# Moving the shift's store and loads to ScalarE's DMA queue, with a new placement of the pieces

## The reference

```
x = x + xattn(layernorm(x), ctx)      # 16 heads of 16: causal self-attention + cross-attention, one output projection
x = x + moe_ffn(layernorm(x))         # 8 experts; each takes the 512 tokens with its highest scores of all 4096
```

## Time and profile before

| | before |
|---|---|
| median of 3 runs | 1600.5 us (1596.9 to 1601.5) |
| the profiled execution | 1592.2 us |
| its span, first to last instruction | 1590.5 us |
| granted TensorE clock, mean | 0.949 |
| PE, DVE, ACT, POOL busy | 91%, 74%, 57%, 34% |
| waits of PE's weight loads for the shift | 31.5 us, 6 times |

### The profile page before, as it was taken

One profiled execution on the slowest core, in us unless ns is written; L12 is line 12 of the kernel. 1 busy time (PEld: TensorE's weight loads), 2 busy tenths in 40 slices (PEclk: granted clock), 3 DMA queues, 4 the chain that ended last, 5 costly groups with the idle time before them and its releaser, 6 DMA issues. The chain is left out here.

```text
span 1590.5 us, 25662 instructions
## 1 busy us (share of the span) xinstructions
PE 1453.4 (91%) x8560; PEld 702.0 (44%) x8560; DVE 1170.5 (74%) x3215; ACT 902.6 (57%) x1754; POOL 547.2 (34%) x1012
## 2 busy tenths in 40 slices
PE   8899999999899899989998999899989856999997
PEld 4443443444344344434443444344433323676674
DVE  6978888878788688879886988687877068455451
ACT  2177777667677677767775677567767600212211
POOL 4032333442344224432533252334113121444442
PEclk8599999999999999999998999899999977999999
DMA  6876473829373855566456736582810120345442
GB/s 176 116 128 106 89 108 103 116 67 142 101 97 87 133 113 87 101 136 106 78 118 127 101 86 110 102 113 70 124 22 3 41 84 14 94 116 122 104 110 51
DMA packets 82388, 155.22 MB, mean 98 GB/s; under 512 B 13008, under 2 KB 46416, under 8 KB 82256
## 3 DMA queue, kind: packets, MB, share of 16 engines
q1 hardware_dynamic: 74752, 142.43, 47.8%
q0 software_dynamic: 6144, 8.52, 3.2%
q10 hardware_dynamic: 1360, 2.62, 0.5%
HBM read 96.52 MB, written 53.08 MB: 94 GB/s over the span
## 5 line engine op out<-in xcount | busy, mean ns | idle before, releaser
L837 ACT ACTIVATE probs<-bank_ps 128x512 f32<-128x512 f32 (+1 forms) x1408 | 719.7, 581 | 273.7 <-PE bank_ps L628 268.9
L943 DVE TENSOR_REDUCE chunk_max<-bank_ps 128x1 f32<-128x512 f32 x1024 | 653.9, 683 | 145.5 <-PE bank_ps L667 142.0
L628 PE MATMUL bank_ps<-q_stack,k_stack 64*128 64x512 f32 (+3 forms) x1536 | 512.9, 428 | 80.0 <-ACT probs L837 49.8
L667 PE MATMUL bank_ps<-k_stack,q_stack 62*128 62x512 f32 (+3 forms) x1536 | 536.1, 438 | 9.3 <-DMA k_stack<-parts 4.8
L667 PEld LDWEIGHTS bank_ps<-k_stack,q_stack 62*128 62x128 f32 x1536 | 253.8, 194 | 357.9 <-DVE chunk_max L943 231.5
L628 PEld LDWEIGHTS bank_ps<-q_stack,k_stack 64*128 64x128 f32 x1536 | 239.7, 190 | 170.1 <-ACT probs L837 133.8
L646 PE MATMUL out_ps<-probs,v_cross 128*32 128x512 f32 x2048 | 276.4, 612 | 0.0
L946 DVE CUSTOM_DVE_ANT_0 masked<-bank_ps,causal 128x128 bf16<-128x128 f32 (+3 forms) x512 | 231.3, 483 | 43.4 <-PE bank_ps L667 40.0
L1142 POOL TENSOR_TENSOR pool_idle<-pool_idle 128x1 f32<-128x1 f32 x292 | 56.5, 193 | 526.0 <-ACT probs L837 328.0
L1475 ACT ACTIVATE h<-h_ps,b1T 128x512 f32<-128x512 f32 x64 | 44.0, 687 | 228.4 <-PE h_ps L1407 228.4
L1183 POOL TENSOR_TENSOR y_sb<-y_sb,y_add 128x256 f32<-128x256 f32 x31 | 22.7, 734 | 293.1 <-DVE y_add L1004 293.1
(11 more groups left out here) (172 smaller groups left out, 1354.4 us busy)
## 6 DMA issues: line engine op xcount, KB each, us to landing
parts_dram<-parts SPq DMA_DIRECT2D x70, 512.0 KB, 2.7
k_stack<-parts_dram SPq DMA_DIRECT2D x180, 192.0 KB, 11.7
q_stack<-parts_dram SPq DMA_DIRECT2D x180, 128.0 KB, 11.0
w1T<-in_L_ffn_fc1s SPq DMA_DIRECT2D x8, 1024.0 KB, 5.7
w2T<-in_L_ffn_fc2s SPq DMA_DIRECT2D x8, 1024.0 KB, 7.3
z_rows<-z_sb SPq DMA_DIRECT2D x8, 528.0 KB, 13.9
x_sb<-in_x SPq DMA_DIRECT2D x8, 512.0 KB, 4.3
ctxT<-in_ctx SPq DMA_DIRECT2D x8, 512.0 KB, 15.3
```

Source lines behind the costliest of these rows:

```text
L628: mm = pe.matmul(bank_of(turn)[:, of.at:of.end], k_stack[base:base + SIDE, g, pair, of.keys:of.keys + P], q_stack[base:base + SIDE, g, pai ...
L667: return pe.matmul(bank[:, 0:n], q_stack[base:base + MAX_ROWS, g, pair, qc:qc + P], k_stack[base:base + MAX_ROWS, g, pair, k0:k0 + n], sta ...
L837: nc.scalar.activation(probs[:, buffer(u, i, p), side, columns], bank_of(("score", g, i, p, side))[:, columns], ACT.Exp, scale=SCALE)\
L943: nc.vector.tensor_reduce(dst, bank[:, 0:n], AX.X, ALU.max).then_inc(max_done, 1)
```

## The change

Three things are changed.

- The shift's store and loads are issued by ScalarE: the store after the exponentials of iteration 8, the loads after those of iteration 9, where ScalarE first waits until the store has landed. Only the very first shift stays with SyncE.
- The common queue loses these steps and what stood around them: nothing holds `fill(0)` or `fill(2)` back until a shift has gone. The wait for the result stores and the residual load move from the end of a batch to the next one, behind `fill(3)`; the last batch also does them at its end.
- PLAN and OUTPUT_PLAN place the pieces and the output steps in other iterations. Each is still done once per batch.

```diff
+SHIFT_STORE = 8
 PLAN = {
-    (0, 2): (("v", 1),), (0, 3): (("vc0", 1),), (0, 5): (("y0T0", 0), ("y0T1", 0)), (0, 6): (("vc1", 1),),
-    (0, 7): (("shift", 0),), (0, 8): (("k", 0),), (0, 9): (("qc", 0),), (1, 1): (("kc1", 0),), (1, 2): (("q", 0),),
-    (1, 4): (("kc0", 0),), (1, 7): (("shift", 0),), (1, 10): (("proj0", 0),), (2, 1): (("proj1", 0),),
-    (2, 4): (("q", 1),), (2, 5): (("v", 0), ("vc0", 0)), (2, 7): (("shift", 0),), (2, 9): (("zT0", 0),),
-    (2, 10): (("kc1", 1), ("zT1", 0)), (3, 2): (("qc", 1),), (3, 3): (("k", 1),), (3, 4): (("kc0", 1), ("vc1", 0)),
-    (3, 6): (("gate", 0),), (3, 7): (("shift", 0),),
+    (0, 2): (("v", 1),), (0, 3): (("vc0", 1),), (0, 5): (("vc1", 1),), (0, 6): (("y0T0", 0), ("y0T1", 0)),
+    (0, 7): (("shift", 0),), (0, 8): (("k", 0),), (0, 9): (("q", 0),), (0, 10): (("kc1", 0),), (1, 1): (("qc", 0),),
+    (1, 2): (("kc0", 0),), (1, 7): (("shift", 0), ("proj0", 0)), (2, 1): (("proj1", 0),), (2, 2): (("q", 1),),
+    (2, 5): (("vc0", 0),), (2, 6): (("vc1", 0),), (2, 7): (("shift", 0),), (2, 8): (("zT0", 0),),
+    (2, 10): (("zT1", 0),), (3, 0): (("kc1", 1),), (3, 2): (("qc", 1),), (3, 3): (("k", 1),), (3, 4): (("kc0", 1),),
+    (3, 6): (("v", 0),), (3, 7): (("shift", 0),), (3, 8): (("gate", 0),),
 }
 OUTPUT_PLAN = {
-    (0, 1): ("turn_cross",), (0, 3): ("divide_cross", "turn_self"), (0, 5): ("divide_self",), (0, 8): ("turn_back",),
-    (1, 0): ("turn_cross",), (1, 2): ("divide_cross", "turn_self"), (1, 4): ("divide_self",), (2, 1): ("turn_cross",),
-    (2, 3): ("divide_cross", "turn_self"), (2, 4): ("divide_self",), (2, 5): ("turn_back",), (3, 1): ("turn_cross",),
-    (3, 2): ("divide_cross", "turn_self"), (3, 4): ("divide_self",),
+    (0, 1): ("turn_cross",), (0, 2): ("divide_cross",), (0, 6): ("turn_self",), (0, 8): ("divide_self",),
+    (0, 9): ("turn_back",), (1, 0): ("turn_cross",), (1, 1): ("divide_cross",), (1, 2): ("turn_self",),
+    (1, 3): ("divide_self",), (2, 1): ("turn_cross",), (2, 2): ("divide_cross",), (2, 4): ("turn_self",),
+    (2, 5): ("divide_self",), (3, 2): ("turn_back",), (3, 4): ("turn_cross",), (3, 5): ("divide_cross", "turn_self"),
+    (3, 8): ("divide_self",),
 }
...
                     fill(3, 2 * b + 2, N_EXP * (4 * b))
+                if b > 1:
+                    stored(b - 1)
+                    load_residual(b - 1)
                 if not last:
                     sp.wait_ge(*freed(find_piece(b, first, last, "vc1", 1)))
                     load_context(b + 1)
-                put_shift(1, 4 * b + 1)
...
                 if not last:
                     project(HALF_ORDER[0], 0)
-                put_shift(2, 4 * b + 2)
...
                     project(HALF_ORDER[1][:EARLY], 1)
-                put_shift(3, 4 * b + 3)
                 if not last:
                     project(HALF_ORDER[1][EARLY:], 1)
-                    put_shift(0, 4 * b + 4)
                     fill(2, 2 * b + 4, N_EXP * (4 * b + 3))
                 if not first:
                     store_results(b - 1, b)
+                if last:
                     stored(b)
                     load_residual(b)
...
+            def store_shift(slot, number):
+
+                act.wait_ge(shift_low, number + 1)
+                act.dma_start(shift_dram[slot % 2].rearrange("t (r q) -> r t q", q=P), shift[:].bitcast(F32))\
+                    .then_inc(shift_out, 16)
+
+            def load_shift(slot, number):
+
+                act.wait_ge(shift_out, 16 * number + 16)
+                rows = shift_dram[slot % 2].rearrange("t (h s n) -> s t h n", s=SIDES, n=Q_COLS)
+                for side in range(SIDES):
+                    act.dma_start(q_stack[SIDE * side + MAX_ROWS:SIDE * side + SIDE, slot].bitcast(F32), rows[side])\
+                        .then_inc(shift_in[slot], 16)
...
                         exp_pair(b, g, i, 1)
+                        if i == SHIFT_STORE and not (last and g == UNITS - 1):
+                            store_shift((g + 1) % UNITS, UNITS * b + g + 1)
+                        elif i == SHIFT_STORE + 1 and not (last and g == UNITS - 1):
+                            load_shift((g + 1) % UNITS, UNITS * b + g + 1)
                         if "turn_back" in outputs_at(first, g, i):
                             add_value_bias(b - (g == 0), int(g == 0))
                         if i == BEHIND - 1 and g > 0:
                             copy_out(b, g - 1, 1)
```

More of the change, by code:

```diff
@@ L506, in fill_directly, with put_first_shift @@
                             .then_inc(landed, 16)
-            def put_shift(slot, number):
-                sp.wait_ge(shift_low, number + 1)
-                sp.dma_start(shift_dram[slot % 2].rearrange("t (r q) -> r t q", q=P), shift[:].bitcast(F32))\
+            def put_first_shift():
+                sp.wait_ge(shift_low, 1)
+                sp.dma_start(shift_dram[0].rearrange("t (r q) -> r t q", q=P), shift[:].bitcast(F32))\
                     .then_inc(shift_out, 16)
-                sp.wait_ge(shift_out, 16 * number + 16)
-                rows = shift_dram[slot % 2].rearrange("t (h s n) -> s t h n", s=SIDES, n=Q_COLS)
+                sp.wait_ge(shift_out, 16)
+                rows = shift_dram[0].rearrange("t (h s n) -> s t h n", s=SIDES, n=Q_COLS)
                 for side in range(SIDES):
-                    sp.dma_start(q_stack[SIDE * side + MAX_ROWS:SIDE * side + SIDE, slot].bitcast(F32), rows[side])\
-                        .then_inc(shift_in[slot], 16)
+                    sp.dma_start(q_stack[SIDE * side + MAX_ROWS:SIDE * side + SIDE, 0].bitcast(F32), rows[side])\
+                        .then_inc(shift_in[0], 16)
             def store_results(n, done):
@@ L579, in _ @@
                 fill_directly(1, pair, False, second_in)
-            put_shift(0, 0)
+            put_first_shift()
             sp.wait_ge(*freed(prologue_piece(PROLOGUE.index(("y0T1", 0)))))
```

## The result

| | before | after |
|---|---|---|
| median of 4 runs | 1598.7 us (1595.7 to 1601.5) | 1640.0 us (1636.7 to 1641.9) |
| span of the profiled execution | 1590.5 us | 1638.6 us |
| granted TensorE clock, mean | 0.949 | 0.934 |

After takes 1.0257 times as long as before (95% interval 1.0229 to 1.0284): 41 us slower. The forecast was 1582.0, its range 1552 to 1607. It was wrong in sign, and what happened is the slower rival B.

What follows compares the result with a forecast made beforehand. TensorE, 91% busy, was taken as the bound, stalled by shifts queued behind fills. From the profiled 1592.2: -46 - 5 + 8 + 24.5 = 1573.7, plus 8.3 for the median, 1582.0 us; own range 1566 to 1600, eight tenths 1552 to 1607.

Steps and rivals of the forecast that it cites:

- rival B: ScalarE's queue waits like the common one, each leg 4.5 us longer beside a fill: +105 us, 1662 us; chance 0.10.
- What bounds the kernel: TensorE is busy 91% of the span; only less idle time or less half-clock time helps; shift stuck behind queued fills.
- Part 1: Six stalls at units 4b+1, batches 2 to 7, and their half-clock stretches go: -46 us, bounds 31.5 to 46.
- Part 2: Pieces placed in other iterations, splitting pairs that shared one: -5 us, bounds -10 to +6.
- Part 3: ScalarE issues one store and two loads in 31 units, delaying its copy and exponentials: +8 us, bounds 0 to some +55.
- rival C: Every issue on ScalarE costs 1.5 us: 1612 us with no collision, about 1600 where half the units see it; chance 0.10.
- rival A: The second queue is served at once, so the collision cost of +24.5 goes: 1557.5 us; chance 0.28.
- Part 4: Shift runs into fill(0) and fill(2) in g = 1 and g = 3: +24.5 us, bounds 0 to 52.
- The price per leg: Extra landing time of the shift's store, and of its loads, on ScalarE's queue beside a full common queue: 1.8 us each.
- the bound of 2.6 us per leg: Upper price for the store's and the loads' delay beside a fill, giving 14 x 3.7 = 52 us.
- Rival D: The stalls don't go, because the engines and not the queue were full at 386.74: 1603 us; chance 0.07.
- The signs named beforehand: What the profile after would show in score-matmul waits, store landings, unit lengths and clock, to tell forecast from rivals.

Runs made afterwards that it cites:

- moved: Kernel before, with only the wait for the result stores and the residual load moved to the next batch, behind fill(3): 1560.7 us, 0.9784 of before.
- moved_plan: As moved, with the new PLAN and OUTPUT_PLAN too, still no shift DMA on ScalarE: 1556.6 us, 0.9743 of before.
- same_queue: Changed kernel with its early fills and new placement, but the shift on the common queue, behind what was issued ahead of it: 1629.7 us (one run).
- act_oldplan: Changed kernel with the old placement of the pieces, shift on ScalarE's queue, fills not held: 1693.7 us (one run).
- hold: Changed kernel, but SyncE begins fill(0) and fill(2) only when that unit's shift loads have landed: 1663.6 us, 1.0424 of before.
- each_out: One fill per unit, shift on ScalarE's queue, but each fill begins when the shift's store has landed, not its loads: 1752.6 us (one run).

## Why the prediction was wrong

**What bounds the kernel** was right: the order on the DMA queues, and the clock behind each stall. The six stalls of the earlier trace rows are gone in after and in `moved`.

**Part 1 (-46)** is 35 us by the move alone, inside the bounds. The prediction asked what is late next on the common queue and answered "nothing". The residual load is: behind `fill(3)` it keeps GpSimd waiting for 87.1 us, GpSimd's masks come late, and TensorE waits for them (17.9 us, 17 times). In batches 2 to 6 that lengthens (0,10) to 3.79 us, (1,0) to 2.88 and (1,1) to 3.82, where batch 1 has 2.74, 2.49 and 3.17 with the same matmuls: 2.1 us, five times, the 10 us that are missing.

**Part 2 (-5)** is 4 us by `moved` and `moved_plan`, no more than their uncertainty, and partly luck: the placement takes GpSimd's late masks off TensorE's path, which part 2 didn't have, and brings new stretches at the lower clock, which it took at nothing.

**Part 3 (+8)** is 7 us, by the two kernels that differ in the issuer alone, with the same reservation. The issues take 0.31 us for the store and 1.2 for the two loads; rival C is out. In quiet units the copy comes at the same place, as the 0.1 us had it.

Parts 1 to 3 together stood at -43. The kernel with one fill per unit, which has all three and no collision, is 0.9669 of before, or -52. Up to here the sum was near: rival A's 1557.5, the price of a changed kernel without collisions, is 13 us above the 1544.8 of that one.

**Part 4 (+24.5, bounds 0 to 52) is the step that failed.** It measures some 95 us, 1640.0 against 1544.8. Of these 7.5 us fall on (3,10) and 4.1 on (1,10), seven times each: 81 us. The other units give the rest: g = 0 takes about 1.4 us more than there (median 39.3 against 37.9) and g = 2 0.7 (35.9 against 35.2), 2.1 a batch or 14 in all, with a clock below 1.00 (0.95 in unit 4 of after) where it is granted in full without the stalls. The price per leg was 1.8 us, chosen from the landings of ScalarE's five stores as if these showed queues that take turns. They are 512 KB each, and nothing in that row tells what was issued before them. The row that did bear on it was in the prediction: the store of the earlier trace rows, issued at 386.74 with a fill and a context load under way, landed 12.4 us later. I read it as the cost of sharing a queue. The same trace gave the right size, too. Part 4 says that the fill begins about 22 us into the unit, takes 18, and that the store comes at 31: by the order of issue that is a wait of 9 us, for which 8.9 to 10.9 were measured. In g = 1 it puts the fill from 15 to 33; in unit 5 of after, which begins at 270.92, it goes from 14.2 to 32.7, and the store, taken at 31 there too, comes at 27.3 (298.24). That makes the wait 5.4 us, and the store landed 5.6 after its issue.

By this the bound of 2.6 us per leg was no bound. The upper end should have been the time until the fill issued before it has landed. The sum's own range, 1566 to 1600, was narrower still than the bounds 0 and 52 that it names as its source.

**Rival B** had the mechanism and nearly the price: 7.5 us in 14 units, 105 us, against 95. It put the wait on each leg. In the trace only the store meets the backlog; the loads go out behind its end and land in 3.0 to 3.6 us. B decides from 3.1 us per colliding unit; the mean was (7.5 + 4.1) / 2 = 5.8 in the two iterations alone. Its chance of 0.10 was too low. One half of what the prediction quoted for it, that a second issuing engine saves only its sequencer's time (the Trainium skill, DMA: Bandwidth & Descriptors, "Issuing engines are not separate DMA queues"), agrees with `same_queue`, 1629.7 against 1640.0 us. The other half says that the DMAs interleave, and not that a small one waits for a whole fill, as the prediction read it. The turns between rings, which the Trainium skill describes in the same page's section "Queues, rings and completion order", didn't take the store past a fill in any run: the 32 KB had to wait for the 1.9 MB on another queue each time, on ScalarE's and on GpSimd's. They may be what let it pass `z_rows`.

**Rival D** is out with `moved`. Its 1603 also left out part 4, which it says remains; with the 24.5 it would have been 1628.

**The signs named beforehand** came out so: no wait of the score matmul (L630) for the shift (yes), ScalarE idle for the store by over 3 us (yes, B), landings of 3 us in g = 1 and 3 (no, 5 to 11), of 1.5 in g = 0 and 2 (yes), half-clock stretches at new places (yes, behind the new stalls, and in four batches behind the gate), short waits of the score matmul for the shift behind g = 3 (no, none: ScalarE is held up first), units 4b + 1 near 36 us (36.2 to 39.9, mean 37.6, for batches 1 to 6).

**What stays open:** why a fill holds the small store back and other bulk transfers don't. Theory F as worded, that a DMA is served behind everything issued before it, is too strong. In after and in `act_oldplan` the store lands 0.2 to 1.8 us before `z_rows` (528 KB), which the common queue had issued 0.1 to 4.1 us ahead of it, in 12 of 12 units. In unit 7 of `act_oldplan` these are `z_rows` at 386.70, `out` at 387.72 and the store at 389.17 (the view's KB and us to landing):
```profile
z_rows<-z_sb SPq DMA_DIRECT2D x1, 528.0 KB, 14.4
out<-x SPq DMA_DIRECT2D x1, 512.0 KB, 14.6
...
shift_dram<-shift ACTq DMA_DIRECT2D x1, 32.0 KB, 10.6
```
They land at 401.1, 402.3 and 399.8, so the store passes a megabyte that is older. The 512 KB loads of `hold` are passed too. A fill's DMAs write 16 partitions each and those transfers move 128; whether that is the reason, or their size, no run tried. The direction alone isn't, since the loads of `hold` come from HBM like a fill. The cost of the lower clock is contained in the unit lengths and was not measured apart.

## What to carry to other kernels

A small transfer on the critical path is best issued before the large ones. Putting it on another engine's queue didn't take it past the fills here: look at what is issued ahead of it on all queues, and take the time until that has landed as its price. It can be less, as past the result stores. What held the bulk transfers back may look like a needless wait; before removing it, see which short transfer goes through the gap that it keeps open, and which later transfer moves when an earlier one does. Where a compute engine issues and waits for such a transfer, its own queue of work stands behind the wait.

## What the runs showed of the hardware

- A 32 KB store on ScalarE's queue, issued while a fill of 1.9 MB was under way on SyncE's, landed 0.2 to 1.3 us behind the fill's last DMA in 14 of 14 units (10.2 us after its issue in unit 7), and 1.46 us after its issue with none under way. None of its packets moved for 7 us in unit 7. On GpSimd's queue it landed 0.2 to 2.9 us behind.
- The same store on ScalarE's queue passed transfers of 512 and 528 KB that the common queue had issued 0.1 to 8.4 us before it: it landed 0.2 to 3.1 us before them (`after`, `act_oldplan`, `hold`).
- A 16 KB load issued in the middle of a fill landed a mean of 1.6 us behind the fill DMAs older than it and 4 to 12 us ahead of the fill's end, in 28 of 28 units of `each_out`, although all of these were on another queue.
- A fill of twelve DMAs lands its first after 3.2 us in the median and its last after 17.4 to 19.7, so one lands every 1.4 us or so, while the issue of all twelve takes 5.4 to 6.6. (The first two fills of the run are slower.)
- GpSimd's own issue takes 0.59 us in the median for the store, against 0.31 on ScalarE and 0.30 on SyncE.
